# GpSimd takes four pieces of elementwise work in a tower of alignment, attention and experts

## The reference

```
h = tok(x, y)                                  # 32 x 128 x 128
h = h + attn(LN(h))   # attn(u) = heads(LN(u)) @ Wm + u
h = h + ffn(LN(h))    # 8 experts, top 2 by gate; silu(u W[e]) * (u V[e]) @ W2[e]
```

## Time and profile before

| | |
|---|---|
| median of 3 runs | 694.59 us (694.49 to 696.78) |
| profiled execution, its own time | 695.72 us |
| its span, first to last instruction | 693.9 us |
| busy: PE / PEld | 370.7 us (53%) / 305.2 us (44%) |
| busy: DVE / ACT / POOL | 496.9 us (72%) / 373.2 us (54%) / 228.7 us (33%) |
| scan stage | to about 221 us |
| attention | about 221 to 458 us |
| expert tiles | about 451 to 667 us, then the final sum and store |

### The profile page before, as it was taken

One profiled execution on the slowest core, in us unless ns is written; L12 is line 12 of the kernel. 1 busy time (PEld: TensorE's weight loads), 2 busy tenths in 40 slices (PEclk: granted clock), 3 DMA queues, 4 the chain that ended last, 5 costly groups with the idle time before them and its releaser, 6 DMA issues.

```text
span 693.9 us, 13468 instructions
## 1 busy us (share of the span) xinstructions
PE 370.7 (53%) x3107; PEld 305.2 (44%) x3108; DVE 496.9 (72%) x1773; ACT 373.2 (54%) x1106; POOL 228.7 (33%) x430
## 2 busy tenths in 40 slices
PE   0400000000000127777767887789999999999930
PEld 0200000000000015555655665678888888888830
DVE  1969999999994578888988977876744444444425
ACT  0434444444442129998977989554455455544510
POOL 1035454545453000000004332465675333333320
PEclk9999999999999998988889979999999999999975
DMA  5177804040324332333250000122332111111129
GB/s 105 45 177 172 178 9 96 4 92 7 88 57 95 106 120 63 108 98 86 74 159 32 23 24 20 53 59 60 81 95 65 41 45 42 45 43 45 39 82 283
DMA packets 113096, 54.06 MB, mean 78 GB/s; under 512 B 56988, under 2 KB 108828, under 8 KB 112947
## 3 DMA queue, kind: packets, MB, share of 16 engines
q1 hardware_dynamic: 106478, 44.53, 26.4%
q0 software_dynamic: 4320, 8.47, 3.7%
q10 hardware_dynamic: 2237, 0.38, 0.4%
HBM read 29.61 MB, written 24.19 MB: 78 GB/s over the span
## 4 chain that ended last, share of the span: by engine, by line
DVE 34%; PE 34%; ACT 13%; issue 8%; DMA 7%; SPq 3%; ACTq 0%; DVEq 0%; POOLq 0%
PE ps L752 9%; PE ps L569 5%; DVE D L1196 5%; DVE D L1205 5%; PE ps L571 5%; PE ps L570 5%; PE ps L742 4%; DVE ps L1185 3%; ACT ps L851 3%; ACT D L857 3%; ACT sq L942 3%; DMA gb<-g_dram 3%; DVE mn L1365 2%; ACT sq L935 2%; DMA iota_sb<-in_iota 2%
## 5 line engine op out<-in xcount | busy, mean ns | idle before, releaser
L1087 POOL DMA_INDIRECT xd_dram<-pay,slot x64 | 62.2, 972 | 212.6 <-DVE pay L1444 185.4
L1108 POOL DMA_INDIRECT y_dram<-ybuf,dest x71 | 69.8, 983 | 100.1 <-DVE ybuf L1550 85.1
L1528 DVE TENSOR_TENSOR sq<-sq,ps 128x512 f32<-128x512 f32 x71 | 48.8, 688 | 70.1 <-PE ps L571 54.6
L605 PE MATMUL ps<-zdiag,ones_f 32*128 32x32 f32 x2 | 0.6, 408 | 181.3 <-DVE zdiag L1273 181.3
L1064 POOL TENSOR_TENSOR D<-D 128x128 f32<-128x128 f32 x130 | 56.2, 432 | 119.2 <-DVE D L1219 59.6
L990 ACT ACTIVATE sq<-ps 128x512 f32<-128x512 f32 x71 | 42.5, 598 | 75.7 <-PE ps L571 75.7
L857 ACT ACTIVATE D<-D 64x2 f32<-64x2 f32 (+1 forms) x154 | 31.3, 204 | 94.6 <-DVE D L1205 78.5
L605 PEld LDWEIGHTS ps<-zdiag,ones_f 32*128 32x128 f32 x2 | 0.5, 308 | 181.4 <-DVE zdiag L1273 181.4
L942 ACT ACTIVATE sq<-sq,mn 128x128 f32<-128x128 f32 x256 | 78.2, 397 | 0.0
L752 PE MATMUL ps<-wdn,xnt 128*128 x568 | 76.2, 277 | 1.9 <-issue 1.2
L752 PEld LDWEIGHTS ps<-wdn,xnt 128*128 128x128 f32 x568 | 69.0, 192 | 4.7 <-issue 4.7
(11 more groups left out here) (222 smaller groups left out, 1062.3 us busy)
## 6 DMA issues: line engine op xcount, KB each, us to landing
stage<-xd_dram SPq DMA_DIRECT2D x71, 65.0 KB
D<-th_dram SPq DMA_DIRECT2D x16, 208.0 KB, 4.0
g_dram<-D SPq DMA_DIRECT2D x14, 208.0 KB, 4.2
x_dram<-D SPq DMA_DIRECT2D x14, 208.0 KB, 4.4
h0q<-g_dram SPq DMA_DIRECT2D x8, 256.0 KB, 3.0
gb<-g_dram SPq DMA_DIRECT2D x8, 256.0 KB, 3.6
xf<-x_dram SPq DMA_DIRECT2D x8, 256.0 KB, 3.2
xb<-x_dram SPq DMA_DIRECT2D x8, 256.0 KB, 3.9
```

Source lines behind the costliest of these rows:

```text
L1087: pool.indirect_dma_start(xd_dram, bass.IndirectOffsetOnAxis(slot[:, q, j, k:k + 1], 0), pay[q % 3][:, k, j, :], None).then_inc(s_sc[2 * k ...
L1108: pool.indirect_dma_start(y_dram, bass.IndirectOffsetOnAxis(dest[:, w:w + 1], 0), yrow[w], None, bounds_check=2 * NB * T - 1, oob_is_err=F ...
```

## The change

The change moves four pieces of work to GpSimd and alters the place of others:

1. `weights`: GpSimd makes both parts of each chunk, in step c-1. ScalarE's and VectorE's pieces are gone.
2. `keys_of_heads`: GpSimd writes `kx` from `qk_k`, in step 4q-4, and PE waits for it by the new semaphore `s_kx`.
3. `inputs_normed`: GpSimd forms h + LN(h) from `h0q` and `hs` in step 4q-9. `hs` becomes double, and `residual` and `load_gauge` wait for it.
4. `copy_inputs`: GpSimd makes the second copy in step 4q+10.
5. Sends: one batch (two indirect DMAs) in each of the steps 4q+16 to 4q+19, and `sent` in 4q+20.
6. ScalarE's `root_first` moves from step 4q-10 to 4q-9, right behind `square`. VectorE's `normalise` moves from 4q+6 to 4q+5, behind `turned`. VectorE's `posterior` moves from 4q-11 to 4q-12.

```diff
             def load_gauge(q):
+                need(sp, s_xn, q - 1)
                 need(sp, s_hx, q - 1)
...
-                pe.wait_ge(s_qk, q + 1)
+                pe.wait_ge(s_kx, q + 1)
...
             for n in STEPS_OF_ATTENTION:     # ScalarE
                 pair(square, n, 2)
+                quad(root_first, n, 9)
...
-                quad(copy_inputs, n, -10)
...
-                quad(root_first, n, 10)
...
-                if 0 <= n + 1 < CHUNKS:
-                    weights_high(n + 1)
...
+            def inputs_normed(q):
+
+                pool.wait_ge(s_hs, q + 1)
+                for k in range(4):
+                    m = pool.tensor_scalar(h1[:, 4 * q + k, :], h0q[q % 2][:, k, :], hs[:, q % 2, 0, k:k + 1],
+                                           hs[:, q % 2, 1, k:k + 1], ALU.mult, ALU.add)
+                m.then_inc(s_hx, 1)
+
+            def weights(c):
+
+                hi, lo, staged = parts_of(c)
+                pool.wait_ge(s_stage[c % 2], 16 * (c // 2 + 1))
+                pool.tensor_copy(hi, staged).then_inc(s_whi, 1)
+                pool.wait_ge(s_whi, c + 1)
+                pool.tensor_tensor(lo, staged, hi.bitcast(f32), ALU.subtract).then_inc(s_wlo, 1)
+
+            def keys_of_heads(q):
+
+                pool.wait_ge(s_qk, q + 1)
+                need(pool, s_d, 4 * q - 4)
+                pool.tensor_tensor(kx[q % 2][:].rearrange("p (h s) -> p h s", s=T), each(qk_k[:], NH),
+                                   over(mask_sb[:], T), ALU.mult).then_inc(s_kx, 1)
+
+            def copy_inputs(q):
+
+                pool.wait_ge(s_x3, q + 1)
+                pool.tensor_copy(pay[q % 3][:, :, 1, 0:E], pay[q % 3][:, :, 0, 0:E]).then_inc(s_x3c, 1)
...
             for n in STEPS_OF_ATTENTION:     # GpSimd
-                quad(sent, n, -18)
-                quad(send_two, n, -16)
-                quad(send_others, n, -17)
+                quad(keys_of_heads, n, 4)
+                quad(sent, n, -20)
+                quad(copy_inputs, n, -10)
+                quad(inputs_normed, n, 9)
+                if n >= 16 and (n - 16) // 4 < NQ:
+                    send((n - 16) // 4, n % 4)
+                if 0 <= n + 1 < CHUNKS:
+                    weights(n + 1)
...
-                for k in range(4):           # VectorE, first_norms
-                    m = V_.tensor_scalar(h1[:, 4 * q + k, :], h[:, k, :], hs[:, 0, k:k + 1], hs[:, 1, k:k + 1],
-                                         ALU.mult, ALU.add)
-                m.then_inc(s_hx, 1)
...
             for n in STEPS_OF_ATTENTION:     # VectorE
                 pair(nearest, n, 2)
-                quad(normalise, n, -6)
...
                 pair(turned, n, 0)
+                quad(normalise, n, -5)
...
-                quad(posterior, n, 11)
+                quad(posterior, n, 12)
...
-                if 0 <= n < CHUNKS:
-                    weights_low(n)
```

More of the change, by code:

```diff
@@ L191, in tower @@
         nwt = sb("nwt", [128, 2, 4])
-        hs = sb("hs", [128, 2, 4])
+        hs = sb("hs", [128, 2, 2, 4])
         mn = sb("mn", [128, 3, NH])
@@ L277, in tower @@
         s_root = sem("s_root")
+        s_hs = sem("s_hs")
         s_hx = sem("s_hx")
@@ L283, in tower @@
         s_qk = sem("s_qk")
+        s_kx = sem("s_kx")
         s_d = sem("s_d")
@@ L428, in sent_rows, with over, each @@
             return 16 * (k // YR + 1) if isinstance(k, int) else k - w + 16
+        def over(a, n):
+            return bass.AP(tensor=a.tensor, offset=a.offset, ap=[a.ap[0], a.ap[1], [0, n]])
+        def each(a, n):
+            return bass.AP(tensor=a.tensor, offset=a.offset, ap=[a.ap[0], [0, n], a.ap[1]])
         CHUNKS = 2 * NX
@@ L956, in numerators @@
                 nc.scalar.activation(ont[q % 2][:, 4 * T:5 * T], ps[:, 1, 0:T], ACT.Copy).then_inc(s_num, 1)
-            def copy_inputs(q):
-                act.wait_ge(s_x3, q + 1)
-                need(act, s_sent, q - 2)
-                nc.scalar.activation(pay[q % 3][:, :, 1, 0:E], pay[q % 3][:, :, 0, 0:E], ACT.Copy).then_inc(s_x3c, 1)
             def inputs(q):
@@ L973, in gates @@
                     nc.scalar.activation(gate[:, 1, :], gate[:, 0, :], ACT.Tanh, scale=0.5).then_inc(s_ex, 1)
-            def weights_high(c):
-                hi, _, staged = parts_of(c)
-                act.wait_ge(s_stage[c % 2], 16 * (c // 2 + 1))
-                nc.scalar.activation(hi, staged, ACT.Copy).then_inc(s_whi, 1)
             def columns(k, c):
@@ L1079, in _, with send @@
             m.then_inc(s_consts, 1)
-            def send(q, pairs):
+            def send(q, k):
                 pool.wait_ge(s_slot, q + 1)
@@ L1084, in send @@
                 pool.wait_ge(s_pay, q + 1)
-                for k in pairs:
-                    for j in range(2):
-                        pool.indirect_dma_start(xd_dram, bass.IndirectOffsetOnAxis(slot[:, q, j, k:k + 1], 0),
-                                                pay[q % 3][:, k, j, :], None).then_inc(s_sc[2 * k + j], 16)
-            def send_two(q):
-                send(q, (0, 1))
-            def send_others(q):
-                send(q, (2, 3))
+                for j in range(2):
+                    pool.indirect_dma_start(xd_dram, bass.IndirectOffsetOnAxis(slot[:, q, j, k:k + 1], 0),
+                                            pay[q % 3][:, k, j, :], None).then_inc(s_sc[2 * k + j], 16)
+            def inputs_normed(q):
[18 more added lines that the diff above has]
+                pool.tensor_copy(pay[q % 3][:, :, 1, 0:E], pay[q % 3][:, :, 0, 0:E]).then_inc(s_x3c, 1)
             def sent(q):
@@ L1275, in _ @@
                                     mz[ends, 0:1], eye_sb[ends, ends], ALU.add, ALU.mult).then_inc(s_zd, 1)
-            def over(a, n):
-                return bass.AP(tensor=a.tensor, offset=a.offset, ap=[a.ap[0], a.ap[1], [0, n]])
-            def each(a, n):
-                return bass.AP(tensor=a.tensor, offset=a.offset, ap=[a.ap[0], [0, n], a.ap[1]])
             dve.wait_ge(s_zp, 1)
@@ L1337, in first_norms @@
                 inverse_roots(0, 2)
-                V_.tensor_scalar(hs[:, 0, :], r1[:, 0, 0, :], 1.0, None, ALU.add)
-                link(V_.scalar_tensor_tensor(hs[:, 1, :], mv[:, 0, :, 0], -1.0, r1[:, 0, 0, :], ALU.mult, ALU.mult))
+                need(dve, s_hx, q - 1)
+                V_.tensor_scalar(hs[:, q % 2, 0, :], r1[:, 0, 0, :], 1.0, None, ALU.add)
+                V_.scalar_tensor_tensor(hs[:, q % 2, 1, :], mv[:, 0, :, 0], -1.0, r1[:, 0, 0, :], ALU.mult, ALU.mult).then_inc(s_hs, 1)
                 need(dve, s_va, q - 1)
@@ L1357, in queries_keys @@
                 V_.tensor_scalar(qs[q % 2][:], qk_x[:], rowc_sb[:, 1:2], rowc_sb[:, 2:3], ALU.mult, ALU.add)
-                link(V_.tensor_scalar(qk_k[:], qk_x[:], rowc_sb[:, 3:4], rowc_sb[:, 4:5], ALU.mult, ALU.add))
-                V_.tensor_tensor(kx[q % 2][:].rearrange("p (h s) -> p h s", s=T), each(qk_k[:], NH),
-                                 over(mask_sb[:], T), ALU.mult).then_inc(s_qk, 1)
+                need(dve, s_kx, q)
+                V_.tensor_scalar(qk_k[:], qk_x[:], rowc_sb[:, 3:4], rowc_sb[:, 4:5], ALU.mult, ALU.add).then_inc(s_qk, 1)
             def nearest(n):
@@ L1383, in residual @@
                 dve.wait_ge(s_rp, q + 1)
+                dve.wait_ge(s_hx, q + 1)
                 b = slice(4 * q, 4 * q + 4)
```

4 lines of the change are left out of this document (removed).

## The result

The changed kernel takes 692.20 us (median of 20 runs, 689.78 to 694.46), the kernel before 694.61 us in as many. The ratio is 0.9963, 95% interval [0.9952, 0.9974]: faster by its interval, but by less than the 0.5% from which on a difference of this kernel counts, and far above the forecast of 669 and its range of 661 to 686. The profiled execution took 691.15 us for a span of 689.3, 4.6 us under the span of before.

What follows compares the result with a forecast made beforehand. VectorE and ScalarE were taken to nearly fill the attention's middle. First quads -4.8, A and B -4.9, C to E -11.7, F to H -4.3 gave -25.7 us: about 669 us, range 661 to 686.

Steps and rivals of the forecast that it cites:

- C to E: Third to fifth of eight four-step attention stretches: 75.42 us falls to 63.7, -11.7, with ScalarE 93% filled.
- its rival at 0.12: VectorE is held while GpSimd reads, 5 us per four steps; C to E gain nothing; 687 us, chance 0.12.
- the earlier trace: Rows before the change: a two-input VectorE instruction starting inside a GpSimd one took its usual 0.30 us, read against holding.
- (c): normalise one step earlier feeds merge in time; VectorE's wait for spread is at most about 1.2 us per quad, hidden.
- The end of attention and the tiles keep their length: After the eight attention stretches, and in the expert tiles (209 us), no time is gained or lost.
- A and B: First two four-step attention stretches: 39.24 us, ScalarE work falling to 31.9, becomes 34.3, -4.9.
- The first quads: Before the first nearest: posterior during the gauge load and h + LN(h) on GpSimd bring it earlier, -4.8 us.
- The share of `posterior`: In the first quads, posterior running during the load: 1.4 us in each of two rounds, plus 1.3 before the first nearest.
- F to H: Last three of eight four-step attention stretches: 66.28 us falls to 62.0 at 89% filling, -4.3.
- GpSimd's prices: Moved pieces on GpSimd: kx 2.14 us, remainder 1.16, copy 0.85, h + LN(h) 1.5; 12.9 us per four steps.
- GpSimd as the bound: Rival: GpSimd's queue in steps -1 to 14 costs 2.5 times the prices; +26, 721 us, chance 0.07.
- The pace of G: Rival: the seventh attention stretch's 22.21 us, PE at lower clock, is the floor; -17.0, 678 us, chance 0.20.

Runs made afterwards that it cites:

- probe_read: Kernel before, with GpSimd adding a spare tile to itself four times in each of steps 0 to 11: 776.43 us, one execution (before 753.8).
- probe_write: Kernel before, with GpSimd filling a spare tile nine times in each of steps 0 to 11, reading nothing: 752.0 us, one execution (before 753.8).
- weights_filled: Changed kernel with earlier posterior and last normalise back, GpSimd filling both weight parts with constants instead of splitting: 725.62 us, 0.9624 of before.
- both: Changed kernel with posterior ahead of queries_keys in its step and the last quad's normalise back in step 34: 685.82 us, 0.9853 of before.
- norm_last_beside: Changed kernel with only the last quad's normalise back in step 34: 735.02 us, 0.9730 of before, beside the changed kernel's 738.30 on that chip.
- moves_only: Changed kernel with weights' parts, kx and h + LN(h) back on ScalarE and VectorE, last normalise in its old step: 685.96 us, 0.9886 of before.
- split_back: Changed kernel with earlier posterior, last normalise back in step 34, and weights' two parts back on ScalarE and VectorE: 684.52 us, 0.9866 of before.
- after_again: The changed kernel unaltered, run again beside the kernel before: 692.11 us, 0.9965 of before.
- timed_sends: Earlier posterior, every normalise in 4q+6, GpSimd chunks after square, sends and sent at old places, against the same without old sends: 748.78 us, 0.9887 of before.

## Why the prediction was wrong, step by step

**"Over C to E this is ... = 13.0 us, which leaves 53.8 of 66.8": the instructions went, the time didn't.** This is the step that failed, with the argument that set its rival at 0.12. VectorE is left with 64.16. So it is VectorE that is fullest, and the term of the sum that stood on ScalarE at 93%, "C to E: 59.2 / 0.93 = 63.7, so -11.7", measured 70.03, -5.4. The rival had said 14 groups in four steps, half a GpSimd instruction each, 5 us. Stretch C shows 1.0 us at L1372, 1.6 at L1319 and 1.4 at L1309 (2.54 for the 1.14 of the earlier trace rows), 4.0 in the three together. The mechanism is shown three ways. Reading by GpSimd alone lengthens rows that no edit touches (probe_read). Without reading it lengthens only the scaled ones, with no stretch longer by over 0.5 us (probe_write). With the split's reading gone C to E fall to the forecast (weights_filled). The rival's time of 687 us is nearer than mine, 5 us under the measured one, and beside `both`, which is without the second loss, it is 1.2 us off. That closeness is partly luck: the rival gave C to E nothing, and they gained 5.4.

**The evidence read wrongly was the earlier trace rows.** They hold one kind of VectorE instruction of 64 elements, begun in the last 0.21 us of a GpSimd one of 0.43. Had it been held, it would have ended 0.18 us later than it did, a margin as large as the doubt about when an instruction's reading ends within its record. The held rows show such a doubt: L1372 of stretch C ends 0.08 us after the subtraction, though it takes 0.34 alone, so by that it went on some 0.26 us before the subtraction's recorded end (an estimate; 0.13 from L1319 in the same way). L1185 began 0.21 us before its end. That may be why this one isn't held; no run shows it. Such a row can't speak for 512 or 1024 elements beside 1.3 to 2.3 us of GpSimd. I named the missing case ("no row here shows the scaled forms") and then gave the rival 0.12 all the same.

**"(c) ... at most the length of PE's products and spread past the transposes, about 1.2 us per quad" and "The end of attention and the tiles keep their length".** Nearly right for the quads in the middle: VectorE waits there in two places, 1.56 and 1.25 us. Wrong for the last quad, whose step 33 holds a tile. PE's queue ahead of `spread` then has the tile's six products and the next tile's transposes, and the wait is 4.74 us. I had counted what stands behind the wait on VectorE for a step of attention, not for the first step with a tile. It costs 6.75 us, with TensorE still at its lower level in the second tile, shown by `both` against the changed kernel, and by norm_last_beside for the wait itself. Of the remaining 2.9 us, 1.3 are the first tile's six products, which take 2.93 us to the `spread` behind them at the lower level, before 1.60; `both` and `moves_only` have them at 2.93 too. Ahead of them PE had stood for 3.17 us at 428.74 (2.9 in `moves_only`). The other 1.6 us lie between the last `nearest` and these products (18.77 us, before 17.20). In them the first rows of the tile table on VectorE (L1481, L1483) stand to the end of GpSimd's `copy_inputs` at 422.72, which costs some 0.8 us; the rest is open.

**A and B: 37.58 for 34.3.** ScalarE is busy 34.35 us in them, not 31.9. B has one more ScalarE instruction than before (55) though four high parts are gone, so others moved in from the neighbouring stretches. A stretch between two marks doesn't keep its contents when the engines shift against each other. In weights_filled A and B are still 35.7, so part of this miss has nothing to do with the standing.

**"The end of attention and the tiles keep their length", for the tiles.** The 70 tiles behind the first take 1.4 us more than before. `moves_only`, `both` and split_back have 1.3, 1.8 and 1.9, spread over the stage, so it belongs to what all four share: the moves, the sends or the second copy. Which, no run separates.

**What was right.** The first quads: 4.2 of 4.8 us. The share of `posterior`, 4.1, measured 4.2 when it was put back. The other shares were not as forecast, 1.2 for h + LN(h) less at most 1 for `kx`: the changed kernel reaches its first `nearest` at 251.84 (251.47 in after_again), `moves_only`, with both on VectorE, at 251.38, so they come to nothing or a small loss. F and G to the last `nearest`: 4.2, forecast 4.3 for F to H. GpSimd's prices: 2.19 for 2.14 (`kx`; 1.89 where nothing meets it), 1.27 for 1.16 (remainder), 0.73 for 0.85 (copy), 2.1 for 1.5 (h + LN(h)); 11.4 to 12.6 us in four steps of B to D, 12.9 forecast. So GpSimd as the bound falls: it has 40 to 54% of B to D free. The Trainium skill, GPSIMD Engine Reference, section 3.1, which has 769 ns for 512 elements in the best loop, is closer to the mean here, 0.73 us, than my 0.85; the shortest, 603 ns, lies under its best. The pace of G as a floor falls, too: in weights_filled the stretches C to E are 0.7 to 1.4 us shorter than G was. That the sends cost nothing by their place isn't shown: see the 1.4 us of the tiles, and timed_sends, where the old place costs 10.7 us on its chip.

**The net.** Forecast -25.7: first quads -4.8, A and B -4.9, C to E -11.7, F to H -4.3. Measured: -4.2, -1.7, -5.4, -4.2, and +9.6 and +1.4 behind them: -4.5. C to E fell 6.3 us short, which is put down to the standing by weights_filled, and the last `normalise` took 6.75.

The best kernels of the study are `both` (0.9853), split_back (0.9866) and moves_only (0.9886), which can't be told apart; each is faster than before and than the changed kernel. In the two latter the weights' split stays on ScalarE and VectorE.

## What to carry to other kernels

Before work is moved from VectorE to GpSimd, count what VectorE still reads from SBUF with two operands or scales there. While GpSimd reads, those stand nearly to its end, and they are counted as busy. Here 29.5 us were taken off and 20.5 came back in rows that nobody had edited. It showed only in their mean times. A moved wait is to be placed in every step in which it occurs, the first and the last above all, with the queue of the engine that it waits for. A rival isn't refuted by a row that is shorter than the effect that it speaks of.

## What the runs showed of the hardware

- Standing goes both ways: h + LN(h) on GpSimd takes 442 to 1126 ns for 128 elements beside VectorE's `xn`, which keeps its 341. GpSimd's copy of a chunk takes up to 1071 ns, 603 at least.
- It isn't in proportion to size. An instruction of 8 elements that begins with a reading of GpSimd of 1.1 us takes 1035 ns, another 167 (probe_read).
- A copy on GpSimd, with one input, holds VectorE too: in `both` a VectorE cast of 8 elements begins at 423.76, inside `copy_inputs` (423.69 to 424.30), and takes 0.56 us instead of 0.17.
- A GpSimd fill holds the scaled forms of VectorE, by 0.16 to 0.29 us each in the mean, and not those with two SBUF inputs of 128 elements and more (probe_write).
- Minimum over 1024 elements (1.21 to 1.22 us), moments (276 to 282 ns) and the attention's rows that read one operand from PSUM (copy of `pt` 683 to 686 ns, `normalise` 676 to 683, `residual` 677 to 679) kept their mean time in every run whose list has them.
- One program can be 8.7% slower on one chip than on another (694.6 and 754.8 us), and there a change can measure 0.978 where it measures 0.996 on the other. Only kernels on the same chip are comparable.
